# A graph network on one core: the right linear layers made during the carries, residuals added by VectorE, and one wide bias product per block

## The reference

```
L0, two layers:  h = relu(mean over in-edges of h[src] @ Wl + b + h @ Wr)
L1, two layers:  8-head attention over in-edges with q, k, v, then + h @ sw + sb (relu between)
L2:              attention with a bias by edge type; h1 = layernorm(h + att @ Wo + bo);
                 layernorm(h1 + gelu(h1 @ W1 + b1) @ W2 + b2)
L3, two layers:  h = (h + max over in-edges of h[src]) @ W + b (relu between)
```

## Time and profile before

| | |
|---|---|
| median of 3 executions | 7070.68 us (7067.34 to 7076.67) |
| profiled execution, its own time | 7077.87 us |
| its span | 7076.2 us |
| POOL, DVE busy | 5104.6 us (72%), 5068.9 us (72%) |
| PE, ACT busy | 2969.7 us (42%), 2517.5 us (36%) |
| mean granted PE clock | 0.719 of 2.4 GHz |

### The profile page before, as it was taken

One profiled execution on the slowest core, in us unless ns is written; L12 is line 12 of the kernel. 1 busy time (PEld: TensorE's weight loads), 2 busy tenths in 40 slices (PEclk: granted clock), 3 DMA queues, 4 the chain that ended last, 5 costly groups with the idle time before them and its releaser, 6 DMA issues.

```text
span 7076.2 us, 61397 instructions
## 1 busy us (share of the span) xinstructions
PE 2969.7 (42%) x17085; PEld 1745.1 (25%) x17085; DVE 5068.9 (72%) x9301; ACT 2517.5 (36%) x6099; POOL 5104.6 (72%) x5264
## 2 busy tenths in 40 slices
PE   4676759888500000010000010000016989778997
PEld 2444435555300000000000000000014555445554
DVE  7676746676588888888888879999986444444443
ACT  3444422222255555445555535555542000000000
POOL 6777767777477777667777747777764777777776
PEclk9888879999755555555555555555558999889997
DMA  4444436666355555455555545555533666546664
GB/s 140 158 158 160 158 115 200 205 202 202 124 159 160 160 160 160 137 161 160 160 160 158 160 124 158 159 161 160 160 123 111 207 211 209 176 159 205 208 208 154
DMA packets 448554, 1169.65 MB, mean 165 GB/s; under 512 B 109489, under 2 KB 142271, under 8 KB 448200
## 3 DMA queue, kind: packets, MB, share of 16 engines
q1 hardware_dynamic: 239852, 655.38, 26.3%
q0 software_dynamic: 208352, 510.28, 25.8%
HBM read 691.61 MB, written 473.62 MB: 165 GB/s over the span
## 4 chain that ended last, share of the span: by engine, by line
POOL 40%; DVE 21%; issue 17%; DMA 11%; ACT 5%; PE 5%; SPq 0%; DVEq 0%; POOLq 0%; ACTq 0%
POOL arena L1800 40%; DMA arena<-table,near_idx 10%; DVE work L856 4%; DVE work L852 3%; DVE outs L721 3%; ACT outs L1256 2%; DVE pair_ps L816 2%; DVE UA L818 2%; PE banks_ps L1439 1%; PE banks_ps L1492 1%; DVE work L739 1%; DVE arena L749 1%; PE banks_ps L1427 1%; DVE LS L847 1%; DVE MS L822 1%
## 5 line engine op out<-in xcount | busy, mean ns | idle before, releaser
L1800 POOL DMA_INDIRECT arena<-table,near_idx x4894 | 4759.1, 972 | 1618.0 <-issue 1385.3
L1463 PE MATMUL cin_ps<-ident,tails 128*128 128x128 f32 x9 | 2.7, 439 | 3223.1 <-DVE tails L981 3223.1
L1492 PE MATMUL banks_ps<-arena,work 128*128 128x384 bf16 x6750 | 1175.7, 333 | 199.0 <-DMA work<-kept_hots 198.3
L721 DVE SCALAR_TENSOR_TENSOR outs<-outs,fence,arena 128x128 f32<-128x128 f32 x1568 | 554.1, 353 | 886.2 <-DMA arena<-table,near_idx 841.0
L721 DVE SCALAR_TENSOR_TENSOR outs<-outs,same,arena 128x128 f32<-128x128 f32 x1568 | 544.5, 347 | 542.5 <-DMA arena<-table,near_idx 525.7
L1492 PEld LDWEIGHTS banks_ps<-arena,work 128*128 128x128 fp8e4 (+1 forms) x6750 | 656.6, 100 | 688.3 <-DMA work<-kept_hots 175.1
L1203 ACT COPY near_idx<-src_i 128x7 int32<-128x7 int32 x784 | 151.0, 194 | 1848.4 <-DVE outs L721 1843.8
L1463 PEld LDWEIGHTS cin_ps<-ident,tails 128*128 128x128 f32 x9 | 1.5, 212 | 3225.4 <-DVE tails L981 3225.4
L856 DVE TENSOR_TENSOR_SCAN work<-banks_ps,work 128x1024 f32<-128x1024 f32 x336 | 769.6, 2291 | 11.5
L1256 ACT COPY outs<-work 128x896 f32<-128x896 f32 x336 | 602.8, 1794 | 7.5 <-DVE work L856 7.5
L816 DVE TENSOR_TENSOR pair_ps<-pair_ps,arena 128x896 f32<-128x896 f32 x336 | 369.5, 1100 | 190.9 <-DMA arena<-table,near_idx 184.8
(11 more groups left out here) (243 smaller groups left out, 5395.5 us busy)
## 6 DMA issues: line engine op xcount, KB each, us to landing
rows_plain<-outs SPq DMA_DIRECT2D x448, 448.0 KB
work<-kept_hots SPq DMA_DIRECT2D x432, 400.0 KB, 5.4
rows_att<-outs SPq DMA_DIRECT2D x336, 504.0 KB
arena<-table,near_idx POOLq DMA_INDIRECT x4894
kept_hots<-hot_small SPq DMA_DIRECT2D x162, 400.0 KB
table<-arena SPq DMA_DIRECT2D x18, 512.0 KB, 3.0
qtable<-arena SPq DMA_DIRECT2D x33, 256.0 KB, 3.6
table<-H SPq DMA_DIRECT2D x24, 256.0 KB, 2.0
```

The costliest lines, as they stand in the source:

```text
L721: v.scalar_tensor_tensor(out_plain[:, s, j, :], prev, flags[:, bass.ds(first + j, 1)], row, *ops).then_inc(s_agg, 1)
L1492: ins = pe.matmul(pick_bank[u], hot[:, t, :], parts3[:, :, t, :], start=(t == 0), stop=(t == NB - 1))
L1800: pool.indirect_dma_start(dst, None, tab, bass.IndirectOffsetOnAxis(ap=idx, axis=0))\
```

## The change

In the two sum layers the product with the right weights and the bias no longer waits for the aggregated rows. It becomes jobs of its own, `xw0` and `xw1`, which PE makes right after `carry_turns` and which ACT copies to `KN`, the memory of `KEEP` seen as rows. When the left product is there, DVE adds the two (`joined_terms`), and ACT rectifies the sum in place (`rectified_sum`). DVE's order in both stages gets this step.

In the graph stage the product with the identity goes. DVE adds the residual while it takes the result out of PSUM (`with_residual`), in place of ACT's copy. The banks of `wo4` and `down4` are thus released by DVE.

In every linear layer with a bias, one product of up to 512 columns sets the whole bank to the bias before PE waits for the turned rows. It replaces one product of 128 columns per tile.

The diff, cut to its core:

```diff
 PHASES = {
     "start": [[], [], ["T_h0"]],
+    "right0": [["xw0"]],
     "sage1": [["T_agg0"], ["lin0"], ["T_h1"]],
+    "right1": [["xw1"]],
...
+def ordered(phase, *order):
+    for slot in range(NBLK + len(PHASES[phase]) - 1):
+        for stage in order:
             if 0 <= slot - stage < NBLK:
                 yield stage, slot - stage
...
@@ job_plan
-                on_vector = name.startswith("qkv")
-                n = BLOCKS[b][1] - BLOCKS[b][0] if on_vector else 1
+                by_tile = name.startswith("qkv")
+                on_vector = by_tile or name in ("wo4", "down4")
+                n = BLOCKS[b][1] - BLOCKS[b][0] if by_tile else 1
@@ block.vector
+            def joined_terms(name, right, dst, b):
+                b0, b1 = BLOCKS[b]
+                j = JOB[name, b][0]
+                v.wait_ge(s_act, job_end(right, b))
+                v.wait_ge(s_pe, j + 1)
+                ps = bank[j % 4][0:NP, 0:(b1 - b0) * D].rearrange("p (i f) -> p i f", f=D)
+                step(v.tensor_tensor(tiles(dst, b), ps, tiles(KN, b), ALU.add), f"{name}_{b}")
+
+            def with_residual(name, dst, residual, b):
...
+                v.wait_ge(s_pe, j + 1)
+                ps = bank[j % 4][0:NP, 0:(b1 - b0) * D].rearrange("p (i f) -> p i f", f=D)
+                v.tensor_tensor(tiles(dst, b), ps, tiles(residual, b), ALU.add).then_inc(s_evict, 1)
+                v.wait_ge(s_evict, TAKEN[j])
...
-            for stage, b in in_stages("sage1"):
+            for stage, b in ordered("sage1", 0, 1):
                 if stage == 0:
                     joined(0, b, "agg0")
+                else:
+                    joined_terms("lin0", "xw0", H, b)
...
-            for stage, b in out_last("sage2"):
+            for stage, b in ordered("sage2", 4, 3, 2, 0, 5, 1):
                 if stage == 0:
                     joined(1, b, "agg1")
+                elif stage == 1:
+                    joined_terms("lin1", "xw1", T2, b)
...
@@ stages 2 and 7 of "graph"
-                    v.wait_ge(s_act, job_end("wo4", b))
+                    with_residual("wo4", T1, H, b)
                     moments("ffn4", T1, b)
...
-                    v.wait_ge(s_act, job_end("down4", b))
+                    with_residual("down4", T1, T2, b)
                     moments("out4", T1, b)
@@ block.scalar
+            def rectified_sum(name, b, dst):
+                act.wait_ge(s_vec, MARK[f"{name}_{b}"])
+                rows3 = dst[0:NP, BLOCKS[b][0]:BLOCKS[b][1], :]
+                act.activation(rows3, rows3, ACT.Relu).then_inc(s_act, 1)
...
             run_pass(0)
+            for _, b in in_stages("right0"):
+                laid("xw0", b, KN)
...
-                    laid("lin0", b, H, ACT.Relu)
+                    rectified_sum("lin0", b, H)
...
             run_pass(1)
+            for _, b in in_stages("right1"):
+                laid("xw1", b, KN)
...
-                    laid("lin1", b, T2, ACT.Relu)
+                    rectified_sum("lin1", b, T2)
...
-                elif stage == 1:
-                    laid("wo4", b, T1)
...
-                elif stage == 6:
-                    laid("down4", b, T1)
@@ block.tensor
-            def linear(name, b, terms, b_at, xt_name, more=None):
+            def linear(name, b, xt, w_at, xt_name, b_at=None):
                 b0, b1 = BLOCKS[b]
-                ps = open_bank(JOB[name, b][0])
+                ps = open_bank(JOB[name, b][0])[0:NP, 0:(b1 - b0) * D]
+                if b_at is not None:
+                    pe.matmul(ps.rearrange("p (i f) -> p i f", f=D), ones_bf[:, 0:NP],
+                              brow3[:, b_at, :].unsqueeze(1).to_broadcast([3, b1 - b0, D]), start=True, stop=False)
                 pe.wait_ge(s_act, job_end(xt_name, b))
                 for i in range(b0, b1):
-                    acc = ps[0:NP, (i - b0) * D:(i - b0 + 1) * D]
-                    for m, (xt, w_at) in enumerate(terms):
-                        pe.matmul(acc, xt[:, i * NP:(i + 1) * NP], W[:, w_at, :], start=(m == 0), stop=False)
-                    if more is not None:
-                        pe.matmul(acc, ident[0:NP, 0:NP], more[0:NP, i, :], start=False, stop=False)
-                    ins = pe.matmul(acc, ones_bf[:, 0:NP], brow3[:, b_at, :], start=False, stop=True)
+                    ins = pe.matmul(ps[:, (i - b0) * D:(i - b0 + 1) * D], xt[:, i * NP:(i + 1) * NP], W[:, w_at, :],
+                                    start=b_at is None, stop=b_at is None or i == b1 - 1)
                 ins.then_inc(s_pe, 1)
...
             carry_turns(0)
             pe.wait_ge(s_vec, MARK["biases"])
             pe.wait_ge(s_parts, 32)
+            for _, b in in_stages("right0"):
+                linear("xw0", b, KEEP, wi["L0_gnn_W1r"], "T_h0", bi["L0_gnn_b1"])
...
-                    linear("lin0", b, [(aT, wi["L0_gnn_W1l"]), (KEEP, wi["L0_gnn_W1r"])], bi["L0_gnn_b1"], "T_agg0")
+                    linear("lin0", b, aT, wi["L0_gnn_W1l"], "T_agg0")
...
             carry_turns(1)
+            for _, b in in_stages("right1"):
+                linear("xw1", b, KEEP, wi["L0_gnn_W2r"], "T_h1", bi["L0_gnn_b2"])
...
-                    linear("wo4", b, [(aT, wi["L2_gnn_Wo"])], bi["L2_gnn_bo"], "T_att4", H)
+                    linear("wo4", b, aT, wi["L2_gnn_Wo"], "T_att4", bi["L2_gnn_bo"])
```

More of the change, by code:

```diff
@@ L102, in in_stages @@
                 yield stage, slot - stage
+def ordered(phase, *order):
+    for slot in range(NBLK + len(PHASES[phase]) - 1):
+        for stage in order:
+            if 0 <= slot - stage < NBLK:
+                yield stage, slot - stage
 def out_last(phase):
     last = len(PHASES[phase]) - 1
[L109 to L112, removed]
+    return ordered(phase, *reversed(range(last)), last)
 def job_plan():
@@ L1506, in pick_rows @@
                 last = LOOPS - 1
-                pe.wait_ge(s_act, job_end({0: "T_h0", 1: "T_h1", 5: "down4", 6: "lin5"}[k], NBLK - 1))
+                if k == 5:
+                    pe.wait_ge(s_evict, job_end("down4", NBLK - 1))
+                else:
+                    pe.wait_ge(s_act, job_end({0: "T_h0", 1: "T_h1", 6: "lin5"}[k], NBLK - 1))
                 pe.wait_ge(s_vec, MARK[f"parts{k}"])
@@ L1574, in _ @@
                 elif stage == 1:
-                    linear("lin1", b, [(aT, wi["L0_gnn_W2l"]), (KEEP, wi["L0_gnn_W2r"])], bi["L0_gnn_b2"], "T_agg1")
+                    linear("lin1", b, aT, wi["L0_gnn_W2l"], "T_agg1")
                 elif stage == 4:
@@ L1611, in _ @@
                 elif stage == 6:
-                    linear("down4", b, [(aT, wi["L2_gnn_W2"])], bi["L2_gnn_b2"], "up4", T2)
+                    linear("down4", b, aT, wi["L2_gnn_W2"], "up4", bi["L2_gnn_b2"])
             pick_rows(5)
@@ L1619, in _ @@
                 else:
-                    linear("lin5", b, [(aT, wi["L3_gnn_W1"])], bi["L3_gnn_b1"], "T_z5")
+                    linear("lin5", b, aT, wi["L3_gnn_W1"], "T_z5", bi["L3_gnn_b1"])
             pick_rows(6)
@@ L1627, in _ @@
                 elif stage == 1:
-                    linear("lin6", b, [(aT, wi["L3_gnn_W2"])], bi["L3_gnn_b2"], "T_z6")
+                    linear("lin6", b, aT, wi["L3_gnn_W2"], "T_z6", bi["L3_gnn_b2"])
         @block.sync
```

## The result

The changed kernel takes 7053.41 us, median of nine runs (7048.36 to 7054.86), against 7070.68 for the kernel before (nine runs, 7066.71 to 7076.67): ratio 0.9972, 95% interval 0.9963 to 0.998. Forecast was 7051, so it is faster by 17 us, a little more than the bound of 14. The profiled execution took 7052.68 us for a span of 7051.0.

What follows compares the result with a forecast made beforehand. POOL was taken to pace the passes, so only node stages could move, PE bounding sage1 and DVE the last graph stage. Terms -4 - 8.5 + 1 - 3.9 - 3.9 = -19.3 off 7070.68 gave 7051 us, range 7041 to 7066.

Steps and rivals of the forecast that it cites:

- the bound of 14: Whole kernel: 14 us, 0.2% of its time, taken as about what can be told from no change.
- The 25 right products and 7 biases leave the critical part: Sage1: moving them ahead takes 17.4 us at 1.2 GHz off the critical part; the stage gains 4 us.
- some 0.32 for a product and 0.16 for a bias: Sum stages: prices in us at 2.4 GHz, dividing a tile's 0.80 us between two products and a narrow bias.
- The lateness of up to 4 us: Sage1: right products last until 966, the first joined block is there at 962, so its turn is up to 4 late.
- The time in which it waits for ACT's copies, 6.1 us, takes up as much of them: Graph stage: DVE's waits absorb 6.1 of the 9 us of new adds, leaving 2.9.
- one interval: Graph stage: faster feeding of the first four blocks credited for a single interval between blocks, 2 us.
- all adds exposed: Graph stage: DVE's adds all stay on its path, +9 us, total 7059 us; chance 0.1.
- The clock did not stay low: Rival for sage1 and sage2: thinner PE work never lifts the clock to 1.00; sum -8.3, 7062 us; chance 0.2.
- The slower case, banks held by DVE: Graph stage: DVE empties wo4 and down4 banks late, 5 us for each of seven blocks; 7086 us; chance 0.04.
- More than the sum: Rival: fast clock in sage1 and the graph stage keeping its early start, sum -30, 7041 us; chance 0.06.
- What was to show it: Trace signs named beforehand for sage1, sage2, graph and gin stages, such as DVE over 95% busy in an unchanged-length graph stage.

Runs made afterwards that it cites:

- g2: The changed kernel with the right layers alone undone, the right product again behind the left in the same bank: 7059.32 us, ratio 0.9974 to the kernel before.
- g1: The changed kernel with the wide bias alone undone, a narrow bias product behind each tile again: 7080.07 us, ratio 1.0002 to the kernel before.
- g3: The changed kernel with DVE's residuals alone undone, PE's identity products copied out by ACT again: 7054.91 us, ratio 0.9967 to the kernel before.
- f4: The changed kernel with ACT copying the graph stage's products out and DVE adding residuals from memory, on a slower chip: 8294.16 us, ratio 0.9961 to the kernel before.
- f1: The changed kernel itself, unaltered, run on a slower chip: 8292.74 us, ratio 0.9957 to the kernel before there.

## Why the prediction was right, and where its reasons were not

The time came out for two reasons that are not of one kind: the parts for gin1 and gin2 were understood, those for the sum stages were right in size by luck. The sum came out by stage almost as forecast:

| term | forecast | measured |
|---|---|---|
| sage1 | -4 | -4.5 |
| sage2 | -8.5 | -10.5 |
| graph | +1 | +2.0 |
| gin1 | -3.9 | -4.4 |
| gin2 | -3.9 | -4.2 |
| sum | -19.3 | -21.6 |

With the conv stages it is -20.4, with the passes' scatter -25.2 between the two profiled spans, and -17.3 between the medians.

**Gin1 and gin2** were right in mechanism and nearly in size. The 0.93 us a tile was read from the rounds, the product alone was expected at 0.57 and took 0.50, the wide bias went into the wait for the copy, and the turns came 5.14 us apart where 5.2 was given.

**Sage1 and sage2** were right in size and wrong in cause. The step that failed is "The 25 right products and 7 biases leave the critical part", with the prices behind it, "some 0.32 for a product and 0.16 for a bias". I split the 0.80 us of a fast tile between two products and a bias by their own rows. g2 shows 0.47 for the two products without the narrow bias, so the bias was 0.33 and a product 0.24. At 1.2 GHz the tile of 1.35 us was 0.9 of products and 0.47 of bias, not 1.14 and 0.21. A stage of 25 tiles thus lost 8 to 12 us by its biases. That alone brings a block at 1.2 GHz from 7.33 us to 5.46, near the rows' 5, and at the fast clock to their pace, after which the right products, 0.45 us or less each, stand where PE would wait. Undoing them (g2) changed sage1 by -1.7 and sage2 by +0.6; undoing the bias (g1) brought back 3.1 and 10.8. The luck is that the whole tile had been read from the trace and only divided wrongly, and that the change took out both parts. Had it been the right layers alone, the same prices would have forecast a gain in both stages; g1, which has them with narrow biases, is 1.4 us shorter than the kernel before in sage1 and 0.3 longer in sage2. The lateness of up to 4 us did not come either: the right blocks took 14.4 us where 17.4 was given, and the first turn of rows stands right behind them at 961.92.

g1 also shows why the right layers cannot pay with narrow biases. Turn of sage2's first block there, behind its 25 right tiles of 0.94 us:

```profile
1844.62 0.28 PE L1508 MATMUL banks_ps<-brow,ones_bf 3*128 3x128 bf16 x1
1845.56 0.28 PE L1508 MATMUL banks_ps<-brow,ones_bf 3*128 3x128 bf16 x1
1845.77 1.11 PE L1482 MATMUL banks_ps<-ident,arena 128*128 128x128 f32 x4
```

It comes at 1845.77 where the kernel before had it at 1836.72: the products were moved out of the stage and their lateness into it.

**Graph**: right sum, one credit given twice. "The time in which it waits for ACT's copies, 6.1 us, takes up as much of them" holds as long as the bias is narrow: 70.5 + 8.8 - 6.1 = 73.2, and g1 has 73.0. But the wide bias removes the same waits (g3: 1.1 us left, stage 63.9). For the faster feed I had given 2 us, "one interval"; it is worth 6.6 without the adds and nothing beside them (72.5 against 73.0), since DVE is then full throughout. In the changed kernel the adds took what DVE had done early. The rival "all adds exposed" was right for what the adds cost, 8.6 us, and wrong for the stage, because the gain that they ate had been put at 2.

**The rivals.** The clock did not stay low: in sage1 it rose earlier (below), and from 1862 to 1896 in sage2 it was 0.99, though 0.50 while sage2's rows came (1834.1 to 1857.1), as before. It did fall in the graph stage, from 0.77 to 0.62 behind the last fetch (the windows beside g3); whether that cost anything, with DVE full, was not tested. The slower case, banks held by DVE, shows in the trace as 14.4 us of PE's waits and in f4, on the slower chip, as no time. "More than the sum" did not come: sage1 ended at 12.0 us, and the graph stage's earlier start went into the adds.

**What was to show it** did in most points: bf16 products of 512 columns from 947.52, POOL's restart in sage1 9.0 us after the last joined block (986.58 to 995.58) where 10 was given, and the memset after sage2 at 1893.18, 36.1 us behind the last fetch where it had been 46.7, so 10.6 nearer instead of 8. DVE at 28.31 of 30 us in the graph stage is 94%, not the 95% named, and the stage is 2.0 us longer, not unchanged; since DVE had 28.20 before, this sign could not tell the cases apart.

## What to carry to other kernels

A small instruction between large ones is priced by the pitch of the rounds with and without it, not by its own row: here a bias product shown as 0.22 to 0.28 us cost 0.33 to 0.47. When one change has several parts that relieve the same engine, undo each alone: the first one made can bring the stage to the next limit, and the others then move work for nothing or, as DVE's adds here, take back part of the gain. Before work is given to an engine, look for what will be full after the change; the waits it would fill may be gone by then.

## What the runs showed of the hardware

PE's granted clock did not follow its busy share. Windows of 20 us from the arrival of sage1's rows, for the changed kernel, g1 and g2 in turn:

```profile
960.60:980.60 20.00, 11.25 (x71) 9.02 (x70) 4.58 (x8) 6.73 (x13) 15.13 (x17) 0.91 0.31 93
```

```profile
960.60:980.60 20.00, 17.86 (x65) 12.94 (x65) 3.53 (x6) 5.04 (x10) 15.12 (x17) 0.50 0.23 66
```

```profile
962.70:982.70 20.00, 16.60 (x96) 13.36 (x96) 2.85 (x5) 6.35 (x11) 15.12 (x17) 0.79 0.32 93
```

With narrow biases PE was busy for 17.86 of 20 us and stayed at 1.2 GHz; with wide ones it was busy for 11.25 and had 0.91. In the changed kernel the rise came after 12 us of fp32 products with only a wide bias between blocks (the timeline above, 948.05 to 960.03). The Trainium skill, "TensorE: Matmul & The Clock Gate", section "Part 1: The HAM clock gate", makes the level a matter of how busy PE has been; g1's window speaks against reading that off the busy column. The same shows ahead of the graph stage, in the 18 us before its last row fetch, in g3 and in the changed kernel:

```profile
5281.50:5299.50 18.00, 13.18 (x76) 10.48 (x76) 14.79 (x63) 6.93 (x13) 13.77 (x14) 0.85 0.24 57
```

```profile
5269.60:5287.60 18.00, 11.96 (x43) 8.63 (x43) 15.41 (x61) 4.29 (x8) 13.73 (x15) 0.50 0.25 57
```

The products with the identity, 33 instructions more, went with 0.85 instead of 0.50. Part of the 6.6 us that g3's graph stage won over the kernel before may be this clock; no run separates it.

Two chips ran every kernel some 18% slower. The chain of f1 there:

```profile
PE 32%; issue 22%; DVE 16%; POOL 16%; another core or an unknown queue 9%; ACT 4%; DMA 2%; DVEq 1%; SPq 0%; POOLq 0%; ACTq 0%
```

On the first chip the changed kernel's chain has 3% of PE, 18% of issue and 42% of POOL, and no share of another core or an unknown queue. The passes took 8017 us there and 6844 here; what makes them longer is not shown. The wide bias was worth 30 us there and about 20 where the kernel takes 7070 (stages of 227.8 us in g1 against 206.7). Why it is worth more there was not tested.
